# P·v between the two halves of the first scores, a round's first product with w1 one cycle earlier, and z turned at the end of the cycle

## The reference

```python
# 1 tokens: patches of 8, 16 and 32 steps at half-patch stride: 127 + 63 + 31 = 221 tokens a sequence
y = jnp.einsum('bnk,dk->bnd', pt, W) + b + pos + scale_emb[i]      # joined over the three scales -> h
# 2 attention over the 221 tokens, 8 heads of 16, on a layer norm of h
scores = jnp.einsum('bhnd,bhmd->bhnm', q, k) / sqrt(Dh)
attn = softmax(scores);  sa = attn @ v;  h = h + sa @ w_agg.T + b_agg
# 3 mixture of 8 experts, each token's 2 experts given; only the first 1024 of the 16*221 tokens take part
for e in range(8): y = where(bin_ids == e, gelu(xg @ w1[e]) @ w2[e], y)
out = zeros.at[token_ids].add(w * y);  h = h + out
```

## Time and profile before

| | us |
|---|---|
| median of 3 runs | 269.61 (268.11 to 270.89) |
| the profiled execution's own time | 267.78 |
| its span, first to last instruction | 266.0 |
| PE busy | 251.3 (94%) |
| DVE busy | 217.1 (82%) |
| ACT busy | 149.4 (56%) |
| POOL busy | 127.9 (48%) |

### The profile page before, as it was taken

How to read it: one execution, slowest core, us unless ns; L and a number is a source line. 1 busy time by engine, 2 the same in 40 slices (tenths; PEclk the granted TensorE clock), 3 DMA queues, 4 the chain that set the end, 5 groups by cost and what they waited for, 6 DMA issues and landing times.

```text
span 266.0 us, 7015 instructions
## 1 busy us (share of the span) xinstructions
PE 251.3 (94%) x2759; PEld 206.8 (78%) x2759; DVE 217.1 (82%) x474; ACT 149.4 (56%) x244; POOL 127.9 (48%) x178
## 2 busy tenths in 40 slices
PE   7999989999899999999999999999999999998991
PEld 7799867777576779887777988888888797876771
DVE  3994679879989989788886979798989898888742
ACT  4770332825261525343437978796969696878350
POOL 4000031103348474748575165667676766855422
PEclk9999999999999999999999999999999999999998
DMA  6999300089301010101111103031313122122122
GB/s 210 418 391 464 130 1 0 2 246 316 90 22 27 28 30 28 27 28 27 30 44 38 40 10 54 19 51 29 51 29 53 27 40 34 16 34 19 30 22 44
DMA packets 17151, 21.30 MB, mean 80 GB/s; under 512 B 2392, under 2 KB 12224, under 8 KB 17088
## 3 DMA queue, kind: packets, MB, share of 16 engines
q1 hardware_dynamic: 12400, 17.68, 20.0%
q0 software_dynamic: 4336, 2.60, 7.9%
q10 hardware_dynamic: 384, 0.57, 0.7%
HBM read 16.44 MB, written 5.95 MB: 84 GB/s over the span
## 4 chain that ended last, share of the span: by engine, by line
PE 65%; DVE 24%; POOL 2%; DMA 2%; ACT 2%; issue 2%; SPq 0%; DVEq 0%; POOLq 0%; ACTq 0%
PE e_ps L1194 12%; PE s_ps L1286 10%; PE s_ps L1194 8%; PE m_ps L1400 7%; PE m_ps L1467 5%; DVE nmax L959 4%; PE m_ps L1268 3%; DVE k_b L935 3%; PE m_ps L1258 2%; PE e_ps L1482 2%; PE e_ps L1467 2%; DMA x_raw<-x 2%; DVE x_lo L821 2%; DVE o_tok L985 1%; PE m_ps L1374 1%
## 5 line engine op out<-in xcount | busy, mean ns | idle before, releaser
L959 DVE TENSOR_REDUCE nmax<-s_ps 128x4 fp32r<-128x884 f32 (+1 forms) x60 | 61.7, 1069 | 8.5 <-PE s_ps L1286 8.3
L632 ACT ACTIVATE probs<-s_ps 128x888 f32<-128x888 f32 (+1 forms) x60 | 51.2, 904 | 20.2 <-PE s_ps L1286 20.2
L527 POOL DMA_INDIRECT out<-y_sb,idx_u x23 | 36.9, 1602 | 26.4 <-DMA out<-y_sb,idx_u 23.5
L465 POOL TENSOR_TENSOR var_eps<-mv,eps_t 128x2 f32<-128x2 f32 x16 | 8.5, 531 | 62.7 <-DVE mv L914 62.6
L498 POOL DMA_INDIRECT z_slots<-z,slot_u x20 | 23.4, 1172 | 15.3 <-PE s_ps L1286 11.0
L1400 PE MATMUL m_ps<-probs,v_aug 128*32 128x221 f32 (+1 forms) x480 | 25.8, 353 | 0.0
L1482 PE MATMUL e_ps<-w_now,hidT 128*128 128x128 f32 x184 | 23.2, 276 | 0.0
L1286 PE MATMUL s_ps<-k_a,q_hi 32*128 32x222 f32 (+1 forms) x252 | 19.1, 309 | 3.7 <-DVE q_lo L929 2.2
L1482 PEld LDWEIGHTS e_ps<-w_now,hidT 128*128 128x128 f32 x184 | 22.4, 192 | 0.1
L1286 PEld LDWEIGHTS s_ps<-k_a,q_hi 32*128 32x128 f32 (+1 forms) x252 | 11.9, 169 | 12.5 <-issue 5.7
L693 ACT ACT_TABLE_LOAD x16 | 20.5, 1283 | 0.3
(11 more groups left out here) (181 smaller groups left out, 602.2 us busy)
## 6 DMA issues: line engine op xcount, KB each, us to landing
w_raw<-wt SPq DMA_DIRECT2D x6, 512.0 KB, 9.8
x_raw<-x SPq DMA_DIRECT2D x6, 512.0 KB, 10.9
w_sb<-w SPq DMA_DIRECT2D x1, 2048.0 KB, 9.7
z_slots<-z SPq DMA_DIRECT2D x1, 1518.0 KB, 15.0
zs<-z_slots SPq DMA_DIRECT2D x7, 198.0 KB, 2.5
x_raw<-x SPq DMA_DIRECT2D x4, 256.0 KB, 5.3
out<-h SPq DMA_DIRECT2D x11, 64.0 KB
c_sb<-consts SPq DMA_DIRECT2D x1, 600.0 KB, 13.1
```

The lines of the kernel that those rows point to most:

```text
L527: g.indirect_dma_start(rows, bass.IndirectOffsetOnAxis(ap=idx_u[:, at:at + 1], axis=0), y_sb[:, n % 2, i, :], None, compute_op=ALU.add).th ...
L632: s.activation(probs[0:n, blk, 2 * f:2 * f + 2].rearrange("p t u n -> p t (u n)"), s_ps[0:n, 2 * f:2 * f + 2, 0:2 * NE], ACT.Exp, scale=DH ...
L959: v.tensor_reduce(nmax[0:n, blk, 2 * f:2 * f + 2, DH:DH + 2], src, AX_X, ALU.max, negate=True).then_inc(max_ready, 1)
```

## The change

Three things are done.

- The tiles of a sequence become 104 and 117 tokens in place of 128 and 93 (`N0 = 104`), with what follows from it in slices and tables.
- On PE, `z_turn` of sequences up to 8 goes to the end of the cycle ahead (`z_turn(c + 2)`, after p4); P·v stands directly between `s1(c, 0)` and `s1(c, 1)`; the p1 tok products go behind `s1(c, 1)`; and `hidden(n + 1, 0)` is issued at the end of cycle n + 7 instead of in cycle n + 8.
- So that the early z does not meet the product with `w_agg` in one bank, `aggregate` of sequences 0 to 5 writes to the upper half of bank 0 of `m_ps` (`agg_bank`). It now waits for `q_ready` in place of `max_in`, the residual also waits for `v_done`, and P·v, which writes over the same columns, waits for the residual of the sequence before (`h1_ready`).

```diff
-N0, N1 = P, N - P
+N0 = 104
+N1 = N - N0
...
+        def agg_bank(b):
+
+            if b == BATCH - 2:
+                return e_ps[:, 2 * P:4 * P]
+            return m_ps[:, 0, 2 * P:4 * P] if b + 3 < LATE_Z else m_ps[:, 2, 0:2 * P]
...
+                if b + 3 < LATE_Z:
+                    dve.wait_ge(v_done, b + 3)
+                v.tensor_tensor(dst, agg_bank(b).rearrange("p (t d) -> p t d", t=2), hb[:, b % 4], ALU.add).then_inc(h1_ready, 1)
...
             def z_turn(b):
 
                 pe.wait_ge(z_ready, b * 2 + 2)
-                if b >= 3:
+                if b >= LATE_Z:
                     pe.wait_ge(h1_ready, b - 2)
...
                 pe.wait_ge(probs_ready, b * 4 + 4)
                 pe.wait_ge(v_ready, b + 2)
+                if b:
+                    pe.wait_ge(h1_ready, b)
...
                 pe.wait_ge(oT_ready, b + 1)
-                if b + 1 < BATCH - 1:
+                bank = agg_bank(b)
+                if b + 3 < LATE_Z:
+                    pe.wait_ge(q_ready, b + 3)
+                elif b + 1 < BATCH - 1:
                     pe.wait_ge(max_in, b + 2)
...
                 if here:
                     s1(c, 0)
-                if ahead1 and c + 1 < LATE_Z:
-                    z_turn(c + 1)
-                if n > 0:
-                    hidden(n, 0)
                 if behind:
                     pv(c - 1)
-                tok_some(p1)
                 if here:
                     s1(c, 1)
+                tok_some(p1)
                 if ahead1 and c + 1 >= LATE_Z:
                     z_turn(c + 1)
...
                 if n < ROUNDS - 1:
                     down(n, 2, ROUND)
+                if n >= 0:
+                    hidden(n + 1, 0)
                 tok_some(p4)
+                if c + 2 < LATE_Z:
+                    z_turn(c + 2)
```

More of the change, by code:

```diff
@@ L401, in store_h1k @@
                 sp.wait_ge(h1_ready, b + 1)
-                sp.dma_start(out[b][0:N0, :], h1k[:, b, 0, :]).then_inc(first_stored, 16)
+                sp.dma_start(out[b][0:N0, :], h1k[0:N0, b, 0, :]).then_inc(first_stored, 16)
                 sp.dma_start(out[b][N0:N, :], h1k[0:N1, b, 1, :]).then_inc(first_stored, 16)
@@ L409, in store_h1 @@
                         sp.wait_ge(y_out[i], 16 * sum(ROUND_TILES[i::2]))
-                sp.dma_start(out[b][0:N0, :], h1[:, b % 2, 0, :]).then_inc(stored[b % 2], 16)
+                sp.dma_start(out[b][0:N0, :], h1[0:N0, b % 2, 0, :]).then_inc(stored[b % 2], 16)
                 if b == BATCH - 1:
@@ L1241, in z_turn @@
                 pe.wait_ge(z_ready, b * 2 + 2)
[L1242 removed]
+                if b >= LATE_Z:
                     pe.wait_ge(h1_ready, b - 2)
[L1244 removed]
+                pe.transpose(m_ps[:, 2, 0:N0], z_sb[0:N0, 0, :], ident[0:N0, 0:N0])
                 pe.transpose(m_ps[:, 2, N0:N], z_sb[0:N1, 1, :], ident[0:N1, 0:N1]).then_inc(z_turned, 1)
@@ L1276, in project_v @@
                     pe.wait_ge(q_ready, b + 1)
-                pe.matmul(m_ps[:, 0, 0:P], zT[:, 0:N0], wqkv_sb[:, 4, :], start=True, stop=True)
+                pe.matmul(m_ps[0:N0, 0, 0:P], zT[:, 0:N0], wqkv_sb[:, 4, :], start=True, stop=True)
                 pe.matmul(m_ps[0:N1, 0, P:2 * P], zT[:, N0:N], wqkv_sb[:, 4, :], start=True,
@@ L1372, in place_max @@
                     n = TILE_N[blk]
-                    w = P if blk == 0 else NE - P
-                    mm = pe.matmul(m_ps[:, 2, P * blk:P * blk + w], nmax[0:n, blk].rearrange("p t r -> p (t r)"),
+                    w = N0 if blk == 0 else NE - N0
+                    mm = pe.matmul(m_ps[:, 2, N0 * blk:N0 * blk + w], nmax[0:n, blk].rearrange("p t r -> p (t r)"),
                                    ident_r[0:n, 0:w], start=True, stop=True)
@@ L1428, in aggregate @@
                     pe.wait_ge(nmaxT_ready, 1)
-                    bank = e_ps[:, 2 * P:4 * P]
-                pe.matmul(bank[:, 0:P], o_T[:, 0:N0], wagg_sb[:], start=True, stop=True)
+                pe.matmul(bank[0:N0, 0:P], o_T[:, 0:N0], wagg_sb[:], start=True, stop=True)
                 pe.matmul(bank[0:N1, P:2 * P], o_T[:, N0:N], wagg_sb[:], start=True, stop=True).then_inc(agg_done, 1)
@@ L1436, in last_aggregate @@
                 pe.wait_ge(probs_ready, 4 * b + 4)
-                pe.matmul(s_ps[:, 0, 0:P], o_T[:, 0:N0], wagg_sb[:], start=True, stop=True).then_inc(agg_done, 1)
+                pe.matmul(s_ps[0:N0, 0, 0:P], o_T[:, 0:N0], wagg_sb[:], start=True, stop=True).then_inc(agg_done, 1)
                 pe.matmul(s_ps[0:N1, 1, 0:P], o_T[:, N0:N], wagg_sb[:], start=True, stop=True).then_inc(agg_done, 1)
@@ L1606, in constants @@
     for b, t in FFN_TILES:
-        token = N * b + P * t + np.arange(P)
+        token = N * b + N0 * t + np.arange(P)
         for k in range(TOP_K):
```

16 lines of the change are left out of this document (6 added, 10 removed).

## The result

The changed kernel takes 277.33 us (median of 4 runs, 276.64 to 278.95) where the kernel before takes 268.86 (4 runs, 268.01 to 270.89): a ratio of 1.031, 95% interval 1.023 to 1.039. (Medians here are over all executions of a kernel; ratios leave out the few that ran in a slower state of the chip.) The prediction had 274.3 and a range up to 276.8, so its sign was right and it fell 3 us short. The profiled execution took 276.77 us with a span of 274.9, 8.9 more than before, where the sum had 4.7.

What follows compares the result with a forecast made beforehand. PE was taken as the bound, busy 94% of the span, so every new wait is paid in full; 2.1 + 0.4 + 0.7 + 0.9 + 0.6 = +4.7 on the 269.61 median gave 274.3 us, range 270.2 to 276.8 (its own 272.4 to 276.6).

Steps and rivals of the forecast that it cites:

- the gap: Between PE's two first-score halves: second half at T (start of `s1(c, 0)`) + 2.87, PE waiting 0.59 for the maxima.
- Cycle 7: `hidden(1, 0)` comes on top of the cycle, with no PE wait before `s1(8, 0)` to absorb it: +0.9 us.
- Rival A: Late cycles really run on DVE, so earlier maxima make the kernel faster: 267.1 us; chance 0.10.
- rival B: Only cycle 0 counts; in later gaps saved neighbours and earlier maxima cancel the wait: 271.7 us; chance 0.22.
- cycles 1 to 6: Terms: 0 in cycles 1 and 6, +0.4 in 2 and 3 together, +0.7 in 4 and 5 together.
- DVE's wait before its second maxima: Sign to look for in the profile after: this wait, 6.5 us in all before, would be gone.
- C: Rival: PE's 2.2 us standstill in cycle 0 drops its clock to 1.2 GHz, +1.5 to +3, 276 to 277; chance 0.06.
- The order's own part: Cycle 0 without any clock change: later second half, 18 tok products behind it, z at the end: +2.1 us.
- cycles 8 to 13: Opened gap and moved w1 product: +0.8 for two openings, +0.2 in 9 to 11, -0.4 in 13; sum +0.6.
- `k_a` ends 0.49 earlier against T: Ends of cycles 9 to 11: the moved w1 product, waiting for `k_a`, can start earlier, costing only +0.1 each.
- the wait for `q_lo`: PE's 0.4 us wait before the next T in cycles 9 to 11, which the moved w1 product was to fill.
- the end: Cycles 14 and 15: chain of additions into the output sets the end and moves with z of cycle 14: 0.

Runs made afterwards that it cites:

- before_apart: Kernel before, only POOL's w1 copies reordered: third tile's ahead of its sum of h and bias, next round's first ahead of a transfer's issue; 265.29 us, ratio 0.989.
- after_w1_back: Changed kernel with each round's first product with w1 back behind the first half of the first scores; 275.27 us, ratio 1.025.
- after_apart: Changed kernel with POOL's w1 copies reordered as in before_apart; 273.95 us, ratio 1.019 to the kernel before.
- after_warm: Changed kernel with 32 products of zeros on PE between the halves of cycle 0's first scores; 279.86 us, ratio 1.044 to the kernel before.
- after_warm8: Changed kernel with 8 products of zeros on PE between the halves of cycle 0's first scores; 274.15 us, ratio 1.023 to the kernel before.
- after_p1_back: Changed kernel with each cycle's first token products back ahead of the second half of the first scores; 273.32 us, ratio 1.017 to the kernel before.
- after_p1_w1_back: Changed kernel with both the first token products and the first product with w1 back in their old places; 268.95 us, ratio 1.002 to the kernel before.
- w1_moved_copy_first: Kernel before with first w1 product at the end of the cycle ahead and POOL's third-tile w1 copy ahead of its sum of h and bias; 270.07 us.
- w1_moved_copies_apart_b: w1_moved_copy_first plus POOL's copy of the next round's first w1 tile ahead of a transfer's issue, apart from the second; 268.12 us, ratio 1.002.
- best_apart_c: Kernel before with the split, z early for sequences 2 to 8, P·v next to the first half, w1 copies as in before_apart; 265.66 us, ratio 0.989.

## Why the prediction was wrong, step by step

**Right: the gap.** `s1(c, 1)` was to come at T + 2.87 after a wait of 0.59; it comes at T + 2.84 after 0.53, in nearly every cycle, and 2.17 in cycle 0. Cycle 7 was to cost 0.9, and it was 0.80. The split costs nothing. Rival A needed PE to have 0.9 us of waiting at a late cycle's start, rival B needed the later gaps to cancel; neither is so. Yet A was right in part: before_apart, which changes only the order of POOL's copies and so shortens DVE's `k_b`, shows that DVE did set the length of most late cycles.

**Luck: cycles 1 to 6.** They were to cost 1.1 and cost 1.08, but the parts are off and cancel. Cycles 2 and 3 cost 0.68 and not 0.4; cycles 4 and 5 cost 0.22 and not 0.7; 1 and 6 cost 0.18 and not 0. One sign also failed: DVE's wait before its second maxima was to be gone, and 4.3 us of it are left. And the range was drawn tighter than its own ends: -2.5 and +2.7 on 274.3 are 271.8 and 277.0, not 272.4 and 276.6.

**Wrong, 1.5 us: the clock in cycle 0.** The sum had nothing for it: the step was not missed but priced as a rival (C, 276 to 277) at a chance of 0.06. The argument against it was that no row showed an idle stretch that long, which is an absence of evidence and no evidence against. The order's own part is 3.41 - 1.51 = 1.9, against 2.1 in the sum. In all four traces that have the 2.17 us open (the changed kernel twice, after_w1_back, after_apart) the clock fell there, and in none where it is filled. All of them also have the 1.2 us for z ahead of it, but so have after_warm, after_warm8, after_p1_back and after_p1_w1_back, so that wait by itself did not do it; whether the 2.17 would without it no run shows. In the changed kernel's first trace the clock fell at 44.08, just behind the 2.17, but in the other three at 42.68, 42.99 and 43.88, while PE still stood (it stood until 44.12, 43.96 and 44.03). It fell for 3.4 us once and for 6.8 three times, with cycle 0 at 15.49 and at 16.38 to 17.02, against 13.98 at full clock. So the changed kernel paid 1.5 and 2.4 us in its two traces, its variants up to 3.0; the 276.77 was one of the cheap executions.

**Wrong, 1.4 us: cycles 8 to 13.** The step that failed is "`k_a` ends 0.49 earlier against T", by which cycles 9 to 11 were to cost 0.1 each. In cycle 11 `k_a` ended at T + 12.99 before (205.92) and ends at T + 12.89 after (211.91): 0.1 earlier, and the cycle costs 0.53. The second half of the scores does come 0.52 earlier; the rest went on the way. The placing comes 3.10 behind the second half instead of 2.88, since the third product waits for POOL's copy of its w1, behind a sum that waits for z (0.2: shown by w1_moved_copy_first, where it is 2.88). Another 0.3 went on DVE's small copy of `slot_w`. The first line is before, the other two after:

```profile
201.14 0.16 DVE L1062 COPY slot_w<-zs 128x3 f32<-128x3 f32 x1
206.93 0.48 DVE L1070 COPY slot_w<-zs 128x3 f32<-128x3 f32 x1
205.11 2.27 POOL L556 COPY w_now<-w_sb 128x512 f32 x3
```

It started 0.30 earlier against T and ended no earlier, with POOL's copies of w2 (207.38). No run moved those copies. But in w1_moved_copies_apart_b, where a copy of w1 takes that place, `slot_w` is held up as well, and `k_a` comes only 0.13 earlier in cycle 11 than in before_apart. (DVE's division, 0.42 us instead of 0.53, gave 0.1 back.) The pair of copies beside `k_b` cost the same in cycle 11 before and after (1.53 and 1.52). In cycle 12 it did not: `k_b` took 0.64 before and takes 1.51 after, and that cycle costs 0.85 and not 0.4. By cycle, 8 to 13 cost 0.04, 0.61, 0.15, 0.53, 0.85 and -0.17, where the sum had 0.4, 0.1, 0.1, 0.1, 0.4 and -0.4. I had written that I take no wait for POOL's copies.

With the copies apart on both sides the move costs 13.60 - 13.17 = 0.43 in every cycle (after_apart against best_apart_c, cycles 9 to 13), near the 0.39 that the sum had for a cycle without the wait for `q_lo`. That wait, which the moved product was to fill, was itself made by the copies beside `k_b`, which took 1.51 us right ahead of the `k_a` of the earlier trace rows; in before_apart `k_b` takes 0.64 and the wait is gone. It was no room that belonged to PE.

**Wrong, 1.6 us: the end.** Cycle 14 gave 0.54 back and the chain of additions took 2.1 more, where the sum had 0 for both. The chain sets the end, as the sum had it; that the chain would only start earlier or later as a whole was the step that failed: the late link alone is 1.95 us longer than before. How much of the 2.1 is chance is open too: in the kernels without the late link this last stretch took 18.5 to 20.8 us (leaving out after_p1_back, whose clock fell there), against 19.4 before and 21.0 to 21.6 with it. Since the late link recurs, it goes with this kernel; since it is absent in both traces with the zeros (3.95 and 4.54 us at that link) and in after_w1_back (4.44), it hangs on timing. In the first trace the bulk of the late transfer moves by 262.0, and 1 to 2 GB/s still move until 263.5. Its cause stays open.

## What to carry to other kernels

Before taking work out of a gap, find the floor of that gap, here the 2.83 us of a half's maxima: work beside a floor is free, and the same work moved to where nothing hides it costs its time, less what the gap shrinks before it meets its floor, even if what looks like a wait stands there. A wait that a trace shows has a cause that may be removable by itself: a `k_b` of 1.5 us among others of 0.64 was a 1% gain, by moving a copy, before any reordering. And on a TensorE-bound kernel an idle stretch costs more than its length when the clock falls behind it; if a new order opens one of 2 us that no trace so far has, measure what it does to the clock, or fill it, before trusting the sum.
